# Graph attention on Trainium2: the row term of the leaky ramp dropped, GpSimd subtracts the ramp's high part from the mask, and VectorE makes all copies of the transposed probabilities

## What is computed

```python
def gat_layer(x, adj, W, a_self, a_neigh, b):        # x [N, F], adj [N, N], 8 heads of 64
    feat = jnp.einsum('nf,hfo->hno', x, W)
    attn_self = jnp.einsum('hno,ho->hn', feat, a_self)
    attn_neigh = jnp.einsum('hno,ho->hn', feat, a_neigh)
    e = jax.nn.leaky_relu(attn_self[:, :, None] + attn_neigh[:, None, :], 0.2)
    e = e + MASK_VAL * (1.0 - adj)[None, :, :]        # MASK_VAL = -1e10
    alpha = jax.nn.softmax(e, axis=-1)
    out = jnp.einsum('hnm,hmo->hno', alpha, feat) + b[:, None, :]
    return jax.nn.elu(jnp.transpose(out, (1, 0, 2)).reshape(out.shape[1], -1))
# per graph, B = 4, N = 512: h = gat_layer(ctx, a, W0, ...); gat_layer(h, a, W1, ...); the result is added to x
...
```

## Time and profile before

| | us |
|---|---|
| median of 3 runs | 2325.42 (2319.11 to 2326.19) |
| the profiled execution | 2323.65, of which the span is 2322.1 |

### The profile page before, as it was taken

One profiled execution on the slowest core, in us unless ns is written; L12 is line 12 of the kernel. 1 busy time (PEld: TensorE's weight loads), 2 busy tenths in 40 slices (PEclk: granted clock), 3 DMA queues, 4 the chain that ended last, 5 costly groups with the idle time before them and its releaser, 6 DMA issues. The chain is left out here.

```text
span 2322.1 us, 35149 instructions
## 1 busy us (share of the span) xinstructions
PE 1861.5 (80%) x8271; PEld 904.7 (39%) x8272; DVE 1542.1 (66%) x3266; ACT 1108.2 (48%) x2014; POOL 586.9 (25%) x701
## 2 busy tenths in 40 slices
PE   1788866888745999999993288888889629999994
PEld 0444433344342555555551122222222414444442
DVE  5988877888766555565563377777776485555552
ACT  1988857888632232232232246666666522222221
POOL 3000012000101555455542211111111003444441
PEclk9799876999876999999996579999999859999997
DMA  4100122001172778889655831111111537988884
GB/s 131 47 37 39 32 79 83 38 1 60 37 230 75 173 174 228 220 182 224 119 100 158 171 57 52 51 51 51 51 51 35 187 104 181 229 230 226 229 213 110
DMA packets 201022, 275.48 MB, mean 119 GB/s; under 512 B 83372, under 2 KB 121740, under 8 KB 199820
## 3 DMA queue, kind: packets, MB, share of 16 engines
q1 hardware_dynamic: 158731, 173.28, 24.3%
q0 software_dynamic: 38544, 97.02, 21.0%
q10 hardware_dynamic: 3633, 3.88, 1.0%
HBM read 204.44 MB, written 73.37 MB: 120 GB/s over the span
## 5 line engine op out<-in xcount | busy, mean ns | idle before, releaser
L1876 DVE TENSOR_REDUCE a_negmax<-a_m 128x1 f32<-128x512 f32 x512 | 328.1, 686 | 101.7 <-PE a_m L1732 100.1
L1824 ACT ACTIVATE a_prob<-a_s 128x1024 f32<-128x1024 f32 x256 | 260.4, 1020 | 142.9 <-PE a_s L1743 137.4
L1268 PE MATMUL f_gu_bank<-f_wgu,f_xT 128*128 x768 | 269.4, 494 | 6.8 <-issue 4.1
L1732 PE MATMUL a_m<-a_kT,a_qT 112*128 (+1 forms) x512 | 198.5, 399 | 82.6 <-DVE a_negmax L1876 39.0
L354 PE MATMUL g_pt<-g_ident,g_p 128*128 128x128 f32 x1024 | 185.6, 311 | 95.6 <-ACT g_p L460 94.2
L1268 PE MATMUL s_gu_bank<-s_wgu,s_xT 128*128 128x512 f32 x512 | 232.0, 596 | 2.3 <-ACT s_xT L1320 1.6
L354 PEld LDWEIGHTS g_pt<-g_ident,g_p 128*128 128x128 f32 x1024 | 127.7, 156 | 239.0 <-issue 151.3
L460 ACT ACTIVATE g_p<-g_e,g_emin 128x512 f32<-128x512 f32 x256 | 184.2, 720 | 66.0 <-DVE g_emin L554 65.9
L1234 POOL DMA_INDIRECT tokens<-f_y,f_ids x96 | 152.1, 1584 | 222.5 <-DMA tokens<-f_y,f_ids 176.6
L544 DVE SCALAR_TENSOR_TENSOR g_l<-g_tb,g_s,g_h 128x512 f32<-128x512 f32 x256 | 190.4, 745 | 17.2 <-ACT g_h L438 17.2
L1268 PEld LDWEIGHTS f_gu_bank<-f_wgu,f_xT 128*128 128x128 f32 x768 | 143.3, 191 | 138.6 <-issue 60.9
(11 more groups left out here) (298 smaller groups left out, 2951.5 us busy)
## 6 DMA issues: line engine op xcount, KB each, us to landing
s_wgu<-in_L_ffn_w_gate_up SPq DMA_DIRECT2D x32, 1024.0 KB, 7.3
f_wgu<-in_L_ffn_gate_up_proj SPq DMA_DIRECT2D x32, 768.0 KB, 5.6
g_tb<-neighbours SPq DMA_DIRECT2D x8, 2048.0 KB
s_wd<-in_L_ffn_w_down SPq DMA_DIRECT2D x32, 512.0 KB, 4.1
a_qT<-q_parts SPq DMA_DIRECT2D x224, 64.0 KB, 2.2
f_wd<-in_L_ffn_down_proj SPq DMA_DIRECT2D x32, 384.0 KB, 5.8
q_parts<-p_part SPq DMA_DIRECT2D x48, 128.0 KB, 2.2
g_mask<-in_x SPq DMA_DIRECT2D x4, 1024.0 KB, 7.7
```

The source lines that it names most:

```text
L1268: last = nc.tensor.matmul(gu_bank[k % TR][:, 0:F], xT[k % TR][:, c, :], wgu[:, bass.ds(place, 1), c, :].rearrange("p a f -> p (a f)"), sta ...
L1732: nc.tensor.matmul(m_bank[n % RING][:, :], qT[k][0:PAIR_ROWS, head, st * P:(st + 1) * P], group_keys(G, PAIR_ROWS, slice(0, N)), start=Tru ...
L1824: nc.scalar.activation(prob[n % QR][:, :, :], s_bank[n % RING][:, :, :], ACT.Exp).then_inc(p_ready, 1)
L1876: V.tensor_reduce(negmax[k % RING][:, st, head:head + 1], m_bank[n % RING][:, :], X_AXIS, ALU.max, negate=True).then_inc(m_read, 1)
```

## The change

- `low` and `s_low` go. The row term -0.2 s is the same for a whole row, and softmax doesn't see it. Its constants in `prepare` (L535) go as well.
- POOL now makes `mless` = mask - high for every unit (`less_high`), up to four units ahead of DVE. `masked` adds t to it: eneg = t_all + mless, again a two-tensor operation on DVE.
- ACT_COPIES is empty: all copies to probT are on DVE, and three units behind (COPY_LAG = 3) instead of two.
- The mask: DVE normalises the tiles of both graphs (8 tiles, one pass). POOL makes (adj - 1) x -1e10 in one pass a tile, four tiles ahead of the units and the other four among units 8 to 11.
- POOL's DMAs for the output blocks are issued between the `less_high` of later units. A store is waited for three units after it was issued.

```diff
-    ACT_COPIES = (0, 2, 4, 6)
-    RELU_AHEAD, LOW_AHEAD = 4, 2
+    ACT_COPIES = ()
+    RELU_AHEAD, COPY_LAG = 4, 3
@@ POOL
-                    pool.wait_ge(rstd_done, i + 1)
-                    ... three passes over graph 1's tiles, then the loop over output blocks
+                    def mask_tile(st):
+                        m = mask[st // NT][:, st % NT, :]
+                        pool.wait_ge(adj_ready, i * (SLOTS * NT) + (st + 1))
+                        pool.tensor_scalar(m, m, -1.0, -1e10, ALU.add, ALU.mult).then_inc(mask_ready, 1)
...
+                    def less_high(n):
+                        k, local = divmod(n, UNITS)
+                        if k < SLOTS and local < NT:
+                            pool.wait_ge(mask_ready, i * (SLOTS * NT) + (k * NT + local + 1))
+                        pool.wait_ge(high_ready, i * ALL_UNITS + (n + 1))
+                        pool.wait_ge(e_ready, i * ALL_UNITS + (n + 1))
+                        pool.tensor_tensor(mless[:, n % LAG, :], mask[k % SLOTS][:, local % NT, :], high[:, n % LAG, :], ALU.subtract).then_inc(mless_ready, 1)
+
+                    for st in range(NT):
+                        mask_tile(st)
+                    for n in range(ALL_UNITS + 3 * PAIR):
+                        if n < ALL_UNITS:
+                            less_high(n)
+                        if 8 <= n < 8 + NT:
+                            mask_tile(NT + n - 8)
+                        j, step = divmod(n - (SLOTS * UNITS + 3 * PAIR), PAIR)
+                        if n == SLOTS * UNITS:
                             for jj in range(RING):
+                                load_old(jj)
+                        if 0 <= j < OUT_PAIRS and step == 4:
+                            store_new(j)
+                        if 0 <= j < OUT_PAIRS and step == 7:
+                            stored(j)
+                            if j + RING < OUT_PAIRS:
+                                load_old(j + RING)
@@ ACT, relu
-                        act.wait_ge(low_ready, i * ALL_UNITS + (n + 1))
+                        act.wait_ge(mless_ready, i * ALL_UNITS + (n + 1))
@@ DVE
-                    for t in range(NT): ... three passes over graph 0's tiles
+                    for st in range(SLOTS * NT):
+                        m = mask[st // NT][:, st % NT, :]
+                        V.tensor_scalar(m, m, mv[:, st, 0:1], rstd[:, st:st + 1], ALU.subtract, ALU.mult).then_inc(adj_ready, 1)
...
-                    def low(n):
-                        ...
-                        V.scalar_tensor_tensor(out=lneg[:, n % LAG, :], in0=t_all[k % SLOTS][:, h, :], scalar=s_low[k % SLOTS][:, t, h:h + 1],
-                                               in1=high[:, n % LAG, :], op0=ALU.add, op1=ALU.subtract).then_inc(low_ready, 1)
...
-                        dve.wait_ge(low_ready, i * ALL_UNITS + (n + 1 + LAG))
+                        dve.wait_ge(mless_ready, i * ALL_UNITS + (n + 1 + LAG))
                         dve.wait_ge(p_ready, i * ALL_UNITS + (n + 1))
-                        V.tensor_tensor_reduce(out=eneg[:, n % LAG, :], in0=lneg[:, n % LAG, :], in1=mask[k % SLOTS][:, local % NT, :],
+                        V.tensor_tensor_reduce(out=eneg[:, n % LAG, :], in0=t_all[k % SLOTS][:, local // NT, :], in1=mless[:, n % LAG, :],
...
                     for n in range(ALL_UNITS + 2 * PAIR):
-                        if n + LOW_AHEAD < ALL_UNITS:
-                            low(n + LOW_AHEAD)
                         if n < ALL_UNITS:
                             masked(n)
-                        if 2 <= n < ALL_UNITS + 2 and (n - 2) % PAIR not in ACT_COPIES:
-                            copy_probT(n - 2)
+                        if COPY_LAG <= n < ALL_UNITS + COPY_LAG and (n - COPY_LAG) % PAIR not in ACT_COPIES:
+                            copy_probT(n - COPY_LAG)
```

More of the change, by code:

```diff
@@ L124, in graph_attention @@
         stT = sb("g_stT", [2 * H, N])
-        s_low = [sb(f"g_s2{i}", [P, NT, H]) for i in range(SLOTS)]
         s_high = [sb(f"g_s8{i}", [P, NT, H]) for i in range(SLOTS)]
@@ L161, in graph_attention @@
         rstd_done = sem("rstd_done")
-        mask_done = sem("mask_done")
+        adj_ready = sem("adj_ready")
+        mask_ready = sem("mask_ready")
         xt_ps = sem("xt_ps")
@@ L255, in _ @@
                 pool.sem_inc(ident_done, 1)
[L256 removed]
+                pool.sem_inc(mless_ready, LAG)
                 with pool.Fori(0, TURNS) as i:
[L259 to L290 removed]
@@ L500, in _ @@
                 with dve.Fori(0, TURNS) as i:
-                    chain.loop(i, 2 * NT * SLOTS + 3 * NT)
+                    chain.loop(i, 2 * NT * SLOTS)
                     for st in range(SLOTS * NT):
@@ L515, in _ @@
                     dve.sem_inc(turns_dve, 1)
-                    for t in range(NT):
-                        chain.mark(V.tensor_scalar(mask[0][:, t, :], mask[0][:, t, :], mv[:, t, 0:1], rstd[:, t:t + 1], ALU.subtract, ALU.mult))
-                    chain.wait()
-                    for t in range(NT):
-                        chain.mark(V.tensor_scalar(mask[0][:, t, :], mask[0][:, t, :], -1.0, 1.0, ALU.mult, ALU.add))
-                    chain.wait()
-                    for t in range(NT):
-                        chain.mark(V.tensor_scalar(mask[0][:, t, :], mask[0][:, t, :], 1e10, None, ALU.mult))
-                    chain.wait()
+                    for st in range(SLOTS * NT):
+                        m = mask[st // NT][:, st % NT, :]
+                        V.tensor_scalar(m, m, mv[:, st, 0:1], rstd[:, st:st + 1], ALU.subtract, ALU.mult).then_inc(adj_ready, 1)
                     def prepare(k, n):
@@ L594, in _ @@
                         prepare(0, n)
-                    for n in range(LOW_AHEAD):
-                        low(n)
                     for n in range(ALL_UNITS + 2 * PAIR):
-                        if n + LOW_AHEAD < ALL_UNITS:
-                            low(n + LOW_AHEAD)
                         if n < ALL_UNITS:
                             masked(n)
-                        if 2 <= n < ALL_UNITS + 2 and (n - 2) % PAIR not in ACT_COPIES:
-                            copy_probT(n - 2)
+                        if COPY_LAG <= n < ALL_UNITS + COPY_LAG and (n - COPY_LAG) % PAIR not in ACT_COPIES:
+                            copy_probT(n - COPY_LAG)
                         if n >= 2 * PAIR:
```

56 lines of the change are left out of this document (17 added, 39 removed).

## The result

The changed kernel takes 2348.57 us (2340.44 to 2354.7). The kernel before, run beside it, takes 2324.06 (2319.11 to 2326.19). The ratio is 1.0106, with a 95% interval from 1.0071 to 1.0142: it is slower, where 2306 was forecast. The profiled execution took 2347.29 us, its span 2345.7 against 2322.1. The graph stage ended at 663.2 us instead of 641.0, so 22.2 of the 23.6 us lie in it.

A forecast was written before the change was run, and what follows sets the result against it. DVE was taken to bound the light phases, PE units 40 to 63. From 2323.65 us, 15 for two turns' faster pace and 4 for the mask gave 2304.6 profiled, forecast as 2306 (2290 to 2318), chance 0.40.

The forecast's parts named there:

- What bounds the kernel: Graph stage: DVE bounds phases 0 and 3, a tenth lost waiting for PE; PE sets the pace in units 40 to 63.
- the PE-bound units 40 to 63: Stretch where PE also prepares a layer 1 phase; little to win, 53.0 us before and 52.2 after.
- The prices of single instructions: POOL's subtraction 1.22 us start to start, 1.27 alone; copies stay 0.69; masked about 1.1 to 1.3 beside POOL.
- The issues of DMAs on POOL: Output-block DMAs in POOL's loop: 0.75 us an issue, 0.19 a unit; the waits for stores costed at nothing.
- The mask: Mask preparation: DVE does 8 tile passes instead of 12, g_stT comes earlier; 2 us a turn, 4 in all.
- The pace of the taken turns: POOL's subtraction and DVE's SBUF-only operations alternate: 1.22 + 0.52 a unit, 14.7 us per eight units, 1.84 a unit.
- the two small operations: zmax and the output operation, SBUF-only on DVE, add 0.25 + 0.50 us per eight units to the taken turns.
- B: Rival, chance 0.20: POOL's and DVE's turns overlap more, PE is the next bound; 1.64 us a unit, 2273 us.
- Rival A: Chance 0.25: POOL's SBUF turns set a slower pace, full 1.27 and 0.61 plus hand-overs, 2.0 a unit; 2350 us.
- POOL over 85% busy: Sign that the forecast is right: POOL's busy share in phases 0 and 3, at 1.84 to 1.92 us a unit.

The follow-up runs named there:

- once in four: Changed kernel with eight places for high and mless, POOL waiting for DVE once in four units: 2352.87 us; with output-block DMAs on SyncE's queue too: 2346.38 us.

## Why the prediction was wrong

**What bounds the kernel** was right. DVE bounds the light phases, before and after, and the PE-bound units 40 to 63 moved by -0.7 us in the first turn and +0.6 in the second, against -0.8 forecast.

**The prices of single instructions** were right. POOL's subtraction was put at 1.22 us from start to start and 1.27 alone; undisturbed it lasts 1.27, and three in a row take 3.71, so 1.22 from start to start. The Trainium skill's "GPSIMD Engine Reference", section 3.1, counts some 2.6 cycles an element for a tensor_tensor; at the 1.2 GHz that it reckons with, 512 columns give an estimate of 1.11 us, under the measured one. Copies stayed at 0.68. `masked` was expected at 1.1 to 1.3 us on average and came at 1.18, POOL's at 1.3 to 1.7 and came at 1.33. The issues of DMAs on POOL cost nothing in the changed kernel.

**The mask** was right. g_stT stands 4.83 us behind the first mask pass, against 6.6 in the earlier trace rows; 4 to 5 was forecast. DVE's timeline:

```profile
353.34 4.91 DVE L533 TENSOR_SCALAR g_mask<-g_mask,g_mv,g_rstd 128x512 f32<-128x512 f32 x8 [0.16 <-DVE g_rstd L528]
358.17 0.67 DVE L541 TENSOR_SCALAR g_stT<-g_f 16x512 f32<-16x512 f32 x1
```

It is 4.83 in the first turn too (38.55 to 43.38 us), so each turn won 1.8 us here where 2 was said; the first relu came 2.3 us earlier.

**The pace of the taken turns is the step that failed.** It put 1.22 + 0.52 = 1.74 us on a unit and 0.75 us on the two small operations of eight units, 14.7 in all; 17.3 was measured. Two things were wrong in it. The larger, 2.2 of the 2.6 us, is the round itself: 8 x 2.01 = 16.1 in place of 8 x 1.74 = 13.9.

- It let the two engines change over at once and without a gap, as if the next turn of either stood ready. That happens where POOL has not yet used up its lead, in the first units of phase 0. There the round is 1.68 us, a little better than the 1.74 of the sum. DVE's timeline, two `masked`, and POOL's of the same moment:

```profile
79.97 1.15 DVE L551 CUSTOM_DVE_ANT_0 g_e<-g_tb,g_ml 128x512 f32<-128x512 f32 x1
...
81.65 1.16 DVE L551 CUSTOM_DVE_ANT_0 g_e<-g_tb,g_ml 128x512 f32<-128x512 f32 x1
```

```profile
80.53 3.43 POOL L288 TENSOR_TENSOR g_ml<-g_mask,g_h 128x512 f32<-128x512 f32 x2
```

Once the lead is used up, each subtraction starts only behind a `masked`, lies beside the copy and then holds the next `masked` to its own end. The round becomes 0.18 + 1.28 + 0.55 = 2.01. The copy lies beside POOL, as forecast, but no longer for nothing: all copies on DVE cost 30 us. With eight places and no DMA on POOL that gap is partly closed, for 10.7 us of the loss.

- It gave the small operations 0.25 and 0.50. Held, zmax and the output operation come to 1.20 and 1.63 us in place of 0.48 and 0.69: 1.66 us more in eight units. A part of it comes back, since the `masked` behind each runs free (0.63 us at 109.31, 0.68 at 114.05): eight units of phase 0 that take 17.3 us (97.94 to 115.26) lie 1.2 over 16.1, in place of 0.75.

Two slips in the sums stand beside this. 14.7 us for eight units are 1.84 a unit, but phases 0 and 3 were reckoned with 1.87 and 1.92 and no reason given; and B's -9.9 in phase 3 doesn't follow from its 1.72 a unit, which gives -8.8. Neither changes the outcome.

What DVE gained and lost in the whole program can be summed from the groups of both turns, before and then after:

```profile
L544 DVE SCALAR_TENSOR_TENSOR g_l<-g_tb,g_s,g_h 128x512 f32<-128x512 f32 x256 | 190.4, 745 | 17.2 <-ACT g_h L438 17.2
L554 DVE CUSTOM_DVE_ANT_0 g_e<-g_l,g_mask 128x512 f32<-128x512 f32 x256 | 175.4, 686 | 0.0
L562 DVE COPY g_pT<-g_pt 128x512 f32<-128x512 f32 x128 | 88.1, 689 | 28.3 <-PE g_pt L354 28.3
L577 DVE TENSOR_TENSOR g_z<-g_o,g_rall 128x512 f32<-128x512 f32 x32 | 22.0, 688 | 13.5 <-PE g_o L383 13.5
L581 DVE TENSOR_SCALAR g_zmax<-g_z,g_bias_m 128x512 f32<-128x512 f32 x32 | 15.6, 489 | 0.1
L586 DVE SCALAR_TENSOR_TENSOR g_res<-g_zexp,g_zmax 128x512 f32<-128x512 f32 x16 | 11.1, 692 | 2.4 <-ACT g_zexp L473 2.3
L586 DVE SCALAR_TENSOR_TENSOR g_xT<-g_zexp,g_zmax 128x512 f32<-128x512 f32 x16 | 11.1, 692 | 2.8 <-ACT g_zexp L473 2.8
```

```profile
L288 POOL TENSOR_TENSOR g_ml<-g_mask,g_h 128x512 f32<-128x512 f32 x256 | 340.0, 1334 | 203.2 <-DVE g_emin L551 153.2 <-ACT g_h L454 49.6
L551 DVE CUSTOM_DVE_ANT_0 g_e<-g_tb,g_ml 128x512 f32<-128x512 f32 x256 | 298.5, 1168 | 21.1 <-POOL g_ml L288 21.1
L578 DVE TENSOR_SCALAR g_zmax<-g_z,g_bias_m 128x512 f32<-128x512 f32 x32 | 36.0, 1125 | 0.1
L583 DVE SCALAR_TENSOR_TENSOR g_xT<-g_zexp,g_zmax 128x512 f32<-128x512 f32 x16 | 26.1, 1634 | 0.0
L583 DVE SCALAR_TENSOR_TENSOR g_res<-g_zexp,g_zmax 128x512 f32<-128x512 f32 x16 | 22.3, 1397 | 0.4 <-ACT g_zexp L489 0.3
```

| DVE, both turns | us |
|---|---|
| `low` gone, 256 x 0.66 | -169 |
| copies come, 128 x 0.60 | +77 |
| `masked` held, 298.5 - 175.4 | +123 |
| zmax and the output operation held, (36.0 - 15.6) and (26.1 + 22.3 - 22.2) | +47 |
| its waits for PE, ACT and POOL, shorter (at the copies 28.3 to 0, at z 13.5 to 2.5, the rest together 7 less) | -46 |
| mask, fewer passes | -3 |
| sum | +29 |

The stage lost 22. The sum is 7 too high, and I can't place these 7 us; overlaps of neighbouring instructions and the ends of the stage are not in such a ledger. Its sense is plain: the 169 us that DVE was relieved of came back as 170 us of being held, and the copies were paid for only in part by the shorter waits.

**Rival A was right in sign and size, and in the main in its mechanism**, 2350 against 2348.57, with 0.25 as its chance. Its place was the read of SBUF, its price POOL's full 1.27 and a hand-over, 2.0 a unit. Its numbers by phase were +5.5, +4, +2.5 and +2.5; +6.9, +1.5, +2.1 and +3.3 were measured in the first turn, 13.8 against its 14.5. What I held against it, that POOL had given way for only 0.19 us in the earlier trace rows, was one meeting, with a tensor_scalar that lasts 0.54 alone and a POOL that had its next subtraction ready. In the changed kernel's first units, where POOL's next one is ready too, it gives way for 0.46 (1.73 in place of 1.27). The same meeting had another row that did speak: that tensor_scalar took 1.46. I took from it that turns are taken, and not that an engine which is the bound pays for the whole turn of the other.

**"POOL over 85% busy" as a sign of being right** was wrong too: 81%, at a pace slower than forecast. It waits on `masked` for 0.73 us a round. A slow pace with POOL idle for a part of it was not in my forecast, and rival A allowed only for a short hand-over.

**What stays open.** Why a `masked` is held through three subtractions only behind a DMA issue of POOL's isn't known; that it goes with the issue is shown by the two kernels with once in four, with and without it, and by the place of every long one, and no more than that. Whether it is the number of SBUF inputs or the kind of operation that spares the reduction wasn't tested. The 10.7 us of the hand-over and the 23 us of the order of `masked` were not measured in one kernel, so whether they add isn't known either.

## What to carry to other kernels

Before an elementwise operation goes to GpSimd to relieve VectorE, count which operations of VectorE read SBUF alone while it runs, and give each the full length of GpSimd's instruction if VectorE is the bound; here that made a free engine cost a little more than it took over (11 to 12 us), and work that nobody needed cost 93 us. If it has to run there, let VectorE's operations that aren't held lie beside it (here those that read PSUM, and the reduction), and look at the order of the others: where GpSimd waits for the first of them, those behind it go free, and the order alone was worth 23 us here. Reading PE's banks one unit later, with as many banks, was worth 10 us; look for such parts in a change that lost, since the best kernel of this study, 2307.06 us, is the change without its main idea.
